# A kernel of one core: small transposes of the identity added to TensorE's queue at 14 places near its start and 6 near its end

## The reference

```python
x = x + _L0_attn_a_ref(_layernorm(x), ...)   # "A": Q, K, V = sigmoid(4*(norm(x @ W) - 1)); weights from the
                                             # distance of the means of Q and K; weights @ V @ Wo + bo
x = x + _L0_ffn_ref(_layernorm(x), ...)      # "F": silu(x @ wg) * (x @ wu) @ wd, int32 weights / 127, hidden 384
x = x + _L0_attn_b_ref(_layernorm(x), ...)   # "B": causal softmax attention, 16 heads of 64
x = x + _L0_ffn_ref(_layernorm(x), ...)      # "P": the same feed-forward again
return x
```

## Time and profile before

| | |
|---|---|
| median of 3 runs | 353.64 us (353.41 to 353.75) |
| profiled execution, its own time | 353.44 us |
| its span, first to last instruction | 351.3 us |
| TensorE matmuls busy | 321.6 us, 92% |
| VectorE, ScalarE, GpSimd busy | 275.9, 233.6, 199.9 us |
| mean granted TensorE clock | 0.981 |

### The profile page before, as it was taken

How to read it: one execution, slowest core, us unless ns; L and a number is a source line. 1 busy time by engine, 2 the same in 40 slices (tenths; PEclk the granted TensorE clock), 3 DMA queues, 4 the chain that set the end, 5 groups by cost and what they waited for, 6 DMA issues and landing times.

```text
span 351.3 us, 9844 instructions
## 1 busy us (share of the span) xinstructions
PE 321.6 (92%) x3208; PEld 275.6 (78%) x3208; DVE 275.9 (79%) x1092; ACT 233.6 (67%) x784; POOL 199.9 (57%) x265
## 2 busy tenths in 40 slices
PE   1685989999999999999999999999999999999764
PEld 0574877888888888989988888888898988888653
DVE  4556479987989889888988899988988887777353
ACT  2335377988677867786787877686768577876410
POOL 4546186577566766657656766577654474336300
PEclk9999699999999999999999999999999999999996
DMA  7800000000000000000000000000000000000001
GB/s 188 284 1 2 0 1 3 3 2 3 1 2 2 4 0 3 17 1 2 3 18 2 2 2 4 17 2 1 3 17 1 2 3 18 0 5 1 17 0 30
DMA packets 6417, 5.81 MB, mean 17 GB/s; under 512 B 864, under 2 KB 5856, under 8 KB 6368
## 3 DMA queue, kind: packets, MB, share of 16 engines
q1 hardware_dynamic: 6080, 4.99, 4.8%
q10 hardware_dynamic: 288, 0.20, 0.2%
HBM read 4.15 MB, written 1.05 MB: 15 GB/s over the span
## 4 chain that ended last, share of the span: by engine, by line
PE 77%; issue 9%; DVE 6%; POOL 3%; ACT 3%; DMA 1%; POOLq 0%; DVEq 0%; ACTq 0%
PE bank L419 11%; PE bank L258 7%; PE bank L385 7%; PE bank L397 7%; PE bank L349 7%; PE bank L259 7%; PE bank L260 7%; PE bank L328 6%; PE bank L383 6%; PE bank L318 3%; PE bank L319 3%; PE bank L276 2%; PE bank L307 2%; PE bank L299 1%; DMA x<-x_in 1%
## 5 line engine op out<-in xcount | busy, mean ns | idle before, releaser
L761 POOL TENSOR_TENSOR prob<-prob,row_inv 128x256 f32<-128x256 f32 (+1 forms) x128 | 103.1, 826 | 93.5 <-DVE row_inv L677 93.5
L510 ACT ACTIVATE prob<-neg_s,neg_max 128x256 f32<-128x256 f32 x128 | 63.8, 498 | 0.0
L508 ACT ACTIVATE prob<-neg_s,neg_max 128x128 f32<-128x128 f32 x128 | 50.6, 396 | 17.4 <-DVE neg_max L663 16.8
L687 DVE TENSOR_TENSOR qk<-bank,bqk 128x512 f32<-128x512 f32 x64 | 43.7, 683 | 12.6 <-PE bank L260 12.4
L663 DVE CUSTOM_DVE_ANT_0 neg_s<-bank,mask 128x256 f32<-128x256 f32 x128 | 53.6, 419 | 0.0
L419 PE MATMUL bank<-prob_t,v 128*64 128x256 f32 (+1 forms) x512 | 48.7, 332 | 0.7 <-DVE prob_t L670 0.7
L419 PEld LDWEIGHTS bank<-prob_t,v 128*64 128x64 f32 x512 | 31.9, 136 | 20.0 <-ACT prob_t L517 9.1
L661 DVE CUSTOM_DVE_ANT_0 neg_s<-bank,mask 128x128 f32<-128x128 f32 x128 | 36.6, 286 | 9.9 <-PE bank L385 9.3
L517 ACT ACTIVATE prob_t<-bank 128x384 f32<-128x384 f32 x64 | 31.1, 486 | 14.8 <-PE bank L397 14.4
L258 PE MATMUL bank<-rt_hi,wqkv_hi 128*128 128x256 f32 x128 | 39.3, 307 | 0.1
L385 PE MATMUL bank<-qk 64*128 64x256 f32 x256 | 38.7, 377 | 0.0
(11 more groups left out here) (141 smaller groups left out, 795.0 us busy)
## 6 DMA issues: line engine op xcount, KB each, us to landing
wqkv<-wqkv_in SPq DMA_DIRECT2D x3, 512.0 KB, 7.2
x<-x_in SPq DMA_DIRECT2D x8, 128.0 KB, 5.8
out<-x SPq DMA_DIRECT2D x8, 128.0 KB, 1.8
wo<-wo_in SPq DMA_DIRECT2D x1, 512.0 KB, 7.0
wa<-wa_in ACTq DMA_DIRECT2D x1, 192.0 KB, 3.1
wg_i<-wg_in SPq DMA_DIRECT2D x1, 192.0 KB, 3.1
wu_i<-wu_in SPq DMA_DIRECT2D x1, 192.0 KB, 3.2
wd_i<-wd_in SPq DMA_DIRECT2D x1, 192.0 KB, 5.3
```

The costliest lines, as they stand in the source:

```text
L508: nc.scalar.activation(prob[:, r, e, 0:P], neg_s[:, m % 2, e, 0:P], ACT.Exp, bias=neg_max[:, q, 2 * e:2 * e + 1], scale=-1.0, accum_out=ro ...
L510: nc.scalar.activation(prob[:, r, e, P:SC], neg_s[:, m % 2, e, P:SC], ACT.Exp, bias=neg_max[:, q, 2 * e + 1:2 * e + 2], scale=-1.0, accum_ ...
L761: nc.gpsimd.tensor_tensor(pr, pr, inv, ALU.mult).then_inc(p_norm, 1)
```

## The change

Twenty jobs are added to TensorE's queue, `hot0` to `hot13` and `end0` to `end5`. Each issues four transposes of `ident` (128x128, 32-bit). The `hot` jobs write them to the first bank of scores and wait only for `ident` to be ready; the `end` jobs write to the second bank of the transposed probabilities and wait until the last of these was read. None of them signals a semaphore. Nothing else is changed on any engine.

By their places (equal places are sorted by name) they stand: `hot13` down to `hot6`, eight jobs, ahead of everything; `hot4` behind `lntA` 0, ahead of `qkv0` 0; `hot5` between `qkv0` 0 and `qkv1` 0; `hot2` between `gF1` 0 and `gF0` 0; `hot1` between `qkv0` 1 and `mean` 1; `hot0` and `hot3` between `lntB` 0 and `vwo` 1; `end2` between `dnP` 6 and `gP0` 7; `end0` between `gP1` 7 and `gP2` 7; `end1`, `end3`, `end4`, `end5` behind `dnP` 7, TensorE's last job.

```diff
--- before.py
+++ after.py
@@ -65,7 +65,10 @@
     "POOL": {"lnsA": -15.831, "sv": -12.368, "stdp": -12.229, "lnsF": -10.37, "lnsB": -6.436, "bo": -3.819, "lnsP": 11.503},
 }
 ONCE = {
-    "PE": {"bo": -170.387, "pre0": 88.584, "pre1": 113.923},
+    "PE": {"hot13": -441.884, "hot12": -441.874, "hot11": -441.864, "hot10": -441.854, "hot9": -441.844, "hot8": -441.834,
+           "hot7": -441.824, "hot6": -441.814, "hot4": -414.832, "hot5": -414.563, "bo": -170.387, "hot2": -140.869, "hot1": -47.225,
+           "hot0": -33.926, "hot3": -33.926, "pre0": 88.584, "pre1": 113.923, "end2": 276.575, "end0": 623.687, "end1": 746.193,
+           "end3": 1003.0, "end4": 1004.0, "end5": 1005.0},
     "ACT": {"w5": -116.539, "w0": -72.76, "w2": -61.38, "w4": -60.294, "w1": -46.737, "w3": -35.799},
     "DVE": {"bv": -112.022, "bo": -97.152},
     "POOL": {"w2": -81.441, "w4": -80.992, "w0": -62.074, "w5": -48.471, "w1": -2.755, "w3": -0.848},
@@ -334,6 +337,16 @@
                     for u in range(U):
                         last = nc.tensor.matmul(out[:, 0:D], bv_all[:, u, :], wo[:, u, :], start=(u == 0), stop=(u == U - 1))
                     last.then_inc(done, 1)
+                elif job.startswith("hot"):
+
+                    pe.wait_ge(consts, 1)
+                    for _ in range(4):
+                        nc.tensor.transpose(s_banks[0][:, 0:P], ident[:], ident[:])
+                elif job.startswith("end"):
+
+                    pe.wait_ge(pt_sb_b, LAST)
+                    for _ in range(4):
+                        nc.tensor.transpose(t_banks[1][:, 0:P], ident[:], ident[:])
                 elif job in ("pre0", "pre1"):
                     j, b, bank_job = int(job[3]), B - 1, f"out{job[3]}"
                     freed(pe, "sum", U * b + U - 3)
```

## The result

The changed kernel takes 352.69 us (median of 20 executions, 350.00 to 353.73) against 353.62 before (20 executions, 353.37 to 354.08). The ratio is 0.9967 with a 95% interval of 0.9955 to 0.9979: 0.33% faster, where 0.86% was forecast. The sign was right, the size was not: of the forecast's 2.8 us one third came. Its executions also differ among themselves by 3.7 us. The profiled one took 353.04 us, span 350.9, which is near the median. All that is read from it is of this one execution.

What follows compares the result with a forecast made beforehand. TensorE, 77% of the span, was taken to bound the kernel. From the profiled 353.44 us, 0.0 - 0.07 + 0.1 - 2.65 - 0.2 gave -2.8, or 350.6; range 349.4 to 355.2, the forecast's own 349.8 to 351.5.

Steps and rivals of the forecast that it cites:

- Bound and price of a block: TensorE bounds the body; a four-transpose block costs 0.85 us at the low clock level, 0.43 at the high.
- Start, 0.0 with bounds of 0.9: Ten start blocks: late `lntA` offset by faster projections, GpSimd then decides; worth 0.0, bounds -0.9 and +0.9.
- The sum's small term: Start: GpSimd's `sv` begins at 12.0 instead of 12.07; entered in the sum as -0.07.
- Theory A: For e2: clock falls again ahead of the first `aout`, nothing gained or lost, 353.6 within 0.4.
- the favourable bound: Start: -0.9 us, if all of the first `aout` runs at the high level.
- Middle, -2.65: Three blocks around `mean` and `vwo` of batch 1 keep the clock high through 35.14 to 41.14 us: -2.65.
- The block behind `gF1`, +0.1: Block costs 0.43 on TensorE's queue, but the DVE's chain has all but 0.1 of slack: +0.1.
- The end, -0.2: End blocks: between -0.9 (high clock for last `dnP`) and +0.35 (earlier fall, clock up again); -0.2 taken.
- the third rival: As forecast, but at the end the clock falls and stays low, +1.7: about 352.5; chance 0.07.
- The course that I had valued at +0.35: End: clock falls inside `dnP` of batch 6, making the chain 1.67 later, but is up for the last `dnP` (-1.32).
- The first: Rival: transposes don't move the clock, so the change is pure cost: about 355.6, from 354 to 357; chance 0.21.
- The second: Rival: start comes out even, but the middle fall stays because the added work is not enough: about 353.9; chance 0.09.

Runs made afterwards that it cites:

- e8: e7 plus the change's ten start blocks and five more blocks in the 2.4 us wait ahead of the first `aout`: 348.92 us, ratio 0.9870.
- e2: Kernel before the change plus only the ten start blocks: 353.17 us, ratio 0.9993.
- e10: e7 plus the change's block behind `gF1` of batch 0: 350.15 us, ratio 0.9904.
- e7: Kernel before plus three middle blocks, nine in the tail's waits, two ahead of `dnF` 0 and two ahead of `lntB` 0: 349.81 us, ratio 0.9897.
- e9: The changed kernel with its six end blocks replaced by nine in the tail's waits (`lntP`, `gP2`, `dnP` of the last batch): 349.86 us, ratio 0.9894.
- e3: Kernel before the change plus only the six end blocks: 353.30 us, ratio 1.0007.
- e1: Kernel before the change plus only the three middle blocks (12 transposes) around `mean` and `vwo` of batch 1: 351.90 us, ratio 0.9969.
- e6: e1 with two ordinary 32-bit matmuls of the identity per block in place of four transposes: 351.68 us, ratio 0.9962.

## Why the prediction was right and wrong

**Bound and price of a block: right.** Blocks follow at 0.107 us a transpose at the high level (1.04 us for eight, with the last one's way through the pipeline) and at 0.21 at the low one (1.06 us for four, behind `dnP`).

**Start, 0.0 with bounds of 0.9: right in sum.** `lntA` started at 8.20, not near 8.0, and ran at the high level. The first `aout` started at 17.14 and took 2.04 us, as before and as argued: TensorE's wait ahead of it brings the clock down; with that wait filled, in e8, it takes 1.13. The sum's small term did not come: `sv` started at 12.36, not 12.0, but that delayed nothing, for `stdp` started at 16.42 as before (16.41). e2's median of 353.17 lies at the edge of Theory A's 0.4. In its profiled execution the clock rose sooner, `lntA` started at 7.35 and `aout` at 16.30, so 0.8 us were gained at the start, near the favourable bound, but not in the way given for it: `aout` itself still took 2.05 us.

**Middle, -2.65: right in kind, 0.2 too large.** From `lntB` to `x` of the second `aout` it was 41.85 - 33.15 = 8.70 us and is 39.74 - 33.45 = 6.29: 2.41 less. `v1` waits 0.25 us for its bank, where I had given 0.15, and the rest is pipeline.

**The block behind `gF1`, +0.1: too small.** `lntB` starts at 33.45 for 33.15, so 0.3; e10's profile has the same 0.3 against e7's. I had looked at VectorE's slack only; in the changed kernel `dnF` starts behind ScalarE's `t_qkv`, at 27.74 for 27.44. Together the body came 2.1 us earlier, not 2.55.

**The end, -0.2: this is the step that failed.** I had worked out both ends of it, -0.9 and, for the third rival, +1.7, and wrote that no row favoured either of two courses; I took "near the middle" and gave the bad case 7 in 100. In the profile it is +1.7, in the very way that was described for a fall behind the moved idle stretch: inside `dnP` of batch 6, with the block and `gP0` at the low level behind it. I had then let the clock be up again for the last `dnP`. It did come up, near 342, but fell a second time near 345.4, right behind the 1.58 us in which TensorE waits for the last `dnP`. So the step that failed is the term -0.2, which measured +1.7: of the 2.4 us between the forecast and the profile it is 1.9, the body's shortfall 0.45. e9, where the waits ahead of `lntP` and of the last `dnP` are filled as well, shows that the tail holds this time. Which of the two waits matters more stays open, for no run fills one alone. The course that I had valued at +0.35 exists too: in e3's profile the clock falls inside `dnP` of batch 6, is back at 342.5 and stays up for the last `dnP`, and the tail takes 10.36 us, 0.7 more than before. The sixteen transposes behind the last `dnP` cost nothing, as argued: they end at 350.33, inside the span of 350.9.

**What stood behind that step: one profile taken for all.** The clock's falls don't come at the same instant of every execution: three profiles of the same middle show three different low stretches, and the tail took from 9.63 to 11.82 us in seven. My sum took away the dearest of these middles and kept the cheapest of these tails. So the question was not on which side of the idle stretch the fall lies, but in what share of the executions it meets a sparse stretch; and the tail has three of them (2.5, 0.6 and 1.6 us of waits in nine), of which the change fills the second. The same holds for the gain: in the cheaper sort of execution there is 0.7 to 1.2 us to be had in the middle (e2's and e3's profiles) instead of 2.4. The changed kernel's five executions with a mean clock of 0.990 took 350.0 to 351.4 us, where the forecast lay; the four with 0.976 took 353.2 to 353.7. The forecast was the good quarter, not the median. How these executions differ inside is not shown: only the one at 353.04 has a profile.

**The rivals.** The first, transposes that don't move the clock, is refuted by the 32 that raised it (0.66 us for `lntA`'s pair before, 0.38 after) and by e1, whose twelve alone held it. By that, the sentence of the Trainium skill in "TensorE: Matmul & The Clock Gate", Part 4: PE-mode transpose, that transposes don't engage the high state, doesn't hold here, for 32-bit transposes of 128x128. The second, a middle that falls in spite of the blocks, was seen only in e6's profile. The third, at 352.5, was the nearest to the 352.69 measured, and nearly in its own way: the end fell, came up for three microseconds and fell again. I gave it 7 in 100.

## What to carry to other kernels

Filler work that is to hold TensorE's clock pays inside the waits, each of them nearly full, and not beside them: three blocks in the right waits did as much as all twenty, and a block on the path costs most of its length (0.3 of 0.43 us for the one behind `gF1`). Judge such a change by the spread of the executions, not by one profile; if they still differ by microseconds, a wait is probably left open. The mean clock is a weaker sign, for it can read 1.000 over a slow start: e7's profile does, though its first `aout` takes 2.05 us there. And when a kernel's body moves, look at its tail again: whatever came by the clock may now come elsewhere.

## What the runs showed of the hardware

A profile's clock line can read full speed at the start of the span while TensorE is at the low level: the kernel before shows 9 in the first two slices while a transpose there takes 449 ns against 272. Twenty microseconds at the start, in which the durations are those of the low level, were hidden in this way. Transposes of the identity, a matrix that is nearly all zeros, raise the clock (32 of them at the start) and, as far as twelve executions each can tell, hold it as matmuls of the same length on the same matrix do (351.90 and 351.68 us). What I had least expected is that the instants of the falls differ between executions of one kernel (34.3, 33.1 and 35.4 us, or 1.2, 0.6 and 2.1 us behind `lntB`, in three profiles whose middles have the same jobs in the same order), so a place for a filler that is tuned on one profile may be tuned to that execution alone.
